# Turning the differences of the longest attention tiles by DMA, as two fp16 parts, in a fused attention and feed-forward layer

## The chip, the cores and the metric

The kernel runs on one core of a Trainium2 chip. The metric is the time of one execution on the device, in microseconds; the median of the runs counts. TensorE (PE in the profile) multiplies and transposes, VectorE (DVE), ScalarE (ACT) and GpSimd (POOL) do the elementwise work, SyncE (SP) issues most of the DMAs. Each engine runs its own instructions in order and waits on semaphores for the others.

## The reference

One transformer layer with differential attention (two softmax maps a head, of which the second is taken off with a factor), group norm, and a gated feed-forward part with ternary weights. B = 4 batches, T = 1024 positions, D = 512, H = 16 heads over KV = 4 key and value heads, E = 2048. Cut to what is computed:

```python
q1, q2 = rope(q[..., :32]), rope(q[..., 32:])      # of x @ Wq; k1, k2 in the same way of x @ Wk
s1 = einsum('bhtd,bhsd->bhts', q1, k1) * scale + mask
s2 = einsum('bhtd,bhsd->bhts', q2, k2) * scale + mask
diff = softmax(s1) - lam * softmax(s2)
out = einsum('bhts,bhsd->bhtd', diff, v)
out = group_norm(out) * (1 - LAMBDA_INIT)
x = layernorm(x + out @ Wo)
x = layernorm(x + (silu(x @ wu.T) * (x @ wg.T)) @ wd.T)   # wu, wg, wd: ternary
```

## The kernel before

The attention is cut into 512 tiles. Tile n has one head and 128 query positions; t from 0 to 7 says which, so that it sees t + 1 blocks of 128 keys. Sixteen tiles are a chunk (two heads, all t), 32 chunks make 4 batches, and tile 128 is the first of the second batch. The order of t (T_ORDER) puts a long tile (t = 7, 6, 5, 4; n even) beside a short one (n odd). r is 0 or 1, the two heads of a chunk; the tiles n and n + 2 of equal t are a "duo".

A tile goes through these steps: "scores" on PE for both maps (L1086); "minimum" on DVE for each, which copies the negated, masked scores to e1 or e2 and takes the row's extreme (L1443); "exponent" on ScalarE with the row sums (L1220); "factor" on GpSimd (L1368, L1369); "combine" on DVE, e1 + coef x e2 (L1514), the difference; "turn", transposes on PE of each block into a PSUM bank, four at most (L1067), and for r = 1 one more of "wide", the factors of the rows (L1071); "evict" on ScalarE from the bank to dt (L1210, L1213); "values" on PE, for each block one fp32 matmul with vkv for each head of the duo, whose outputs lie in the two halves of a bank (L1105); "product" on DVE (L1535). e1_long, e1_short and dt_short hold more than one tile, e2_long and e2_short one. dt_long has one place for each r.

Beside it run the "fills" on PE, cut into pieces: the projections of x (kinds E, O, V, two pieces each; L1125, L1132), the output projection with Wo (L1146), the transposes of its result (x1T, L1150), and the feed-forward jobs up, gate (L1159) and y (L1168). A batch's output projection and feed-forward part can start when its attention is complete, so those of the last batch stand in a tail behind all attention. The projections of later batches are spread over the time before.

What stands where on an engine is decided by a planner, `in_order`, when the program is built. It has a cost for each step (`takes`), what each step waits for (`after`), how long a DMA takes to land (`LANDS`), a preference (`AHEAD`), a pace (`PACE`: from tile 128 on, scores start no sooner than 16 x PACE after those of 16 tiles before, in the plan's time), and it lays out one fixed list for each engine. SP's list holds the loads of q (qstk, four places), k, v and weights, and the stores.

## Time and profile before

| | us |
|---|---|
| median of 3 runs | 2203.38 |
| lowest, highest | 2203.05, 2204.61 |
| the profiled execution's own time | 2203.33 |
| its span in the profile | 2201.3 |
| PE busy | 2132.3 |
| DVE busy | 1684.0 |
| ACT busy | 1458.0 |
| POOL busy | 1193.6 |

The profile is of one execution. Busy times are of instructions alone, not of waits; a matmul counts with its latency, so that a PE that is called busy may still have small gaps. An fp32 matmul is recorded as two instructions, a transpose or an fp16 matmul as one. Idle time is put down to the instruction of another engine that ended last before it ended.

### The profile page before, as it was taken

What the parts mean: (1) busy time and instruction counts of PE and PEld (TensorE: products, weight loads), DVE (VectorE), ACT (ScalarE), POOL (GpSimd) and SP (SyncE); (2) the same over time, 40 slices, a digit from 0 to 9 for tenths busy, and PEclk for the clock granted to TensorE, in tenths of its full rate; (3) what the DMA queues carried; (4) which work ended last, traced back from release to release, by engine and by line L of the source; (5) the groups of instructions that cost most, each with busy time, mean ns of one, the idle gap of its engine ahead of it and who ended that gap; (6) DMA issues with size and microseconds to landing.
All of it is one profiled execution on the core that took longest, in us unless ns stands there. A gap on an engine that the chain in (4) does not pass through costs nothing. (4 is left out here: it accounts for less than half of the span.)

```text
span 2201.3 us, 41404 instructions
## 1 busy us (share of the span) xinstructions
PE 2132.3 (97%) x13442; PEld 1375.0 (62%) x13442; DVE 1684.0 (77%) x3701; ACT 1458.0 (66%) x3450; POOL 1193.6 (54%) x1919
## 2 busy tenths in 40 slices
PE   8999999999999999999999999999999999999998
PEld 4666666666666666666666666666666666644443
DVE  4888788889889888888878878888877888743333
ACT  0777777667777777778677767767677777722232
POOL 0577666677655745555545655665554555531232
PEclk9999999999999999999999999999999999999999
DMA  7676566857653422222532322342532112021000
GB/s 253 198 211 217 191 213 203 244 174 222 189 164 116 121 72 68 92 59 72 173 115 63 87 68 72 98 130 68 154 92 68 51 42 87 30 77 48 1 20 20
DMA packets 257427, 255.49 MB, mean 116 GB/s; under 512 B 31296, under 2 KB 199360, under 8 KB 255168
## 3 DMA queue, kind: packets, MB, share of 16 engines
q1 hardware_dynamic: 246016, 220.26, 33.3%
q10 hardware_dynamic: 11200, 32.58, 4.6%
q8 instruction: 112, 1.84, 0.4%
q14 instruction: 99, 0.81, 0.1%
HBM read 181.48 MB, written 71.30 MB: 115 GB/s over the span
## 5 line engine op out<-in xcount | busy, mean ns | idle before, releaser
L1368 POOL TENSOR_TENSOR linv<-lsum,powers 128x2 f32<-128x2 f32 x512 | 408.7, 798 | 425.2 <-ACT e_long L1220 341.4
L1220 ACT ACTIVATE e_long<-e_long,nmax 128x768 f32<-128x768 f32 (+3 forms) x512 | 504.9, 987 | 161.2 <-DVE nmax L1443 157.7
L1443 DVE CUSTOM_DVE_ANT_0 e_long<-PS,mask_b 128x768 f32<-128x768 f32 (+3 forms) x512 | 516.2, 1019 | 74.8 <-PE PS L1086 56.3
L1086 PE MATMUL PS<-kstk,qstk 128*128 128x384 f32 (+5 forms) x1536 | 473.2, 413 | 20.9 <-DVE nmax L1443 10.2
L1086 PEld LDWEIGHTS PS<-kstk,qstk 128*128 128x128 f32 x1536 | 269.3, 189 | 143.2 <-issue 79.5
L1210 ACT ACTIVATE dt_long<-PS 128x512 f32<-128x512 f32 (+3 forms) x544 | 259.5, 514 | 121.2 <-PE PS L1067 114.4
L1514 DVE SCALAR_TENSOR_TENSOR e_long<-e_long,coef 128x1024 f32<-128x1024 f32 (+3 forms) x256 | 276.4, 1080 | 82.2 <-POOL coef L1369 81.7
L1220 ACT ACTIVATE e_short<-e_short,nmax 128x384 f32<-128x384 f32 (+3 forms) x512 | 283.0, 557 | 11.4 <-DVE nmax L1443 10.6
L1381 POOL TENSOR_TENSOR hid<-th,hid 128x512 f16<-128x512 f32 x128 | 148.3, 1161 | 251.6 <-ACT hid L1262 131.2
L1369 POOL TENSOR_SCALAR coef<-lsum,linv,neglam 128x1 f32<-128x1 f32 x512 | 229.5, 448 | 53.4
L1067 PE MATMUL PS<-ident,e_long 128*128 128x128 f32 x1664 | 240.5, 276 | 11.3 <-DVE nmax L1443 4.7
L1443 DVE CUSTOM_DVE_ANT_0 e_short<-PS,mask_b 128x384 f32<-128x384 f32 (+3 forms) x512 | 236.7, 485 | 9.9 <-PE PS L1086 4.5
L1168 PE MATMUL PS<-down_t,hid 128*128 128x512 fp8e4 x1024 | 233.9, 379 | 0.0
L1067 PEld LDWEIGHTS PS<-ident,e_long 128*128 128x128 f32 x1664 | 196.4, 142 | 54.3 <-issue 13.8
L1105 PE MATMUL PS<-dt_long,vkv 128*64 128x128 f32 x3328 | 205.0, 274 | 0.0
L1125 PE MATMUL PS<-xT,wr 128*128 128x512 f32 x400 | 190.2, 603 | 7.4 <-DMA wr<-in_w_proj 5.7
L1159 PE MATMUL PS<-x_hi,up_t 128*128 128x512 f16 x512 | 195.3, 381 | 0.0
L1159 PE MATMUL PS<-x_lo,up_t 128*128 128x512 f16 x512 | 194.9, 381 | 0.0
L1159 PE MATMUL PS<-x_hi,gate_t 128*128 128x512 f16 x512 | 194.2, 379 | 0.1
L1159 PE MATMUL PS<-x_lo,gate_t 128*128 128x512 f16 x512 | 194.0, 379 | 0.0
L1210 ACT ACTIVATE dt_short<-PS 128x512 f32<-128x512 f32 (+3 forms) x256 | 121.3, 474 | 105.3 <-PE PS L1071 68.7
L1105 PEld LDWEIGHTS PS<-dt_long,vkv 128*64 128x64 f32 x3328 | 187.7, 138 | 0.3 <-issue 0.3
(125 smaller groups left out, 3345.6 us busy)
## 6 DMA issues: line engine op xcount, KB each, us to landing
qstk<-dq SPq DMA_DIRECT2D x512, 128.0 KB, 2.9
dq<-hl SPq DMA_DIRECT2D x25, 1024.0 KB, 4.9
wr<-in_w_proj ACTq DMA_DIRECT2D x48, 512.0 KB, 4.6
kstk<-dk SPq DMA_DIRECT2D x64, 256.0 KB, 5.1
da<-ra SPq DMA_DIRECT2D x32, 512.0 KB, 3.3
at_sb<-da SPq DMA_DIRECT2D x32, 512.0 KB, 4.1
wt<-in_w_up SPq DMA_DIRECT2D x16, 512.0 KB, 5.9
wt<-in_w_gate SPq DMA_DIRECT2D x16, 512.0 KB, 5.2
```

Source lines behind the costliest of these rows:

```text
L1067: last = nc.tensor.transpose(F[bank][:, k * P:(k + 1) * P], e1_of(n)[:, col:col + P], ident[:, :])
L1086: last = nc.tensor.matmul(slot[:, h, :], qstk[:, duo % 4, 2 * r + m, :].bitcast(F32R), kstk[:, g % 2, m, h * w:(h + 1) * w].bitcast(F32R), ...
L1105: last = nc.tensor.matmul(bank[64 * r:64 * r + 64, at:at + P], vkv[:, duo // 16 % 2, kb, :], dt_of(n)[:, kb, :], start=kb == 0, stop=kb == t)
L1125: last = nc.tensor.matmul(bank[:, :], wr[:, job.i % 2, c, at:at + P], x_part(job, c), start=c == 0, stop=c == DC - 1)
L1159: last = nc.tensor.matmul(bank[:, :], w[:, c, job.i * P:(job.i + 1) * P], part[:, c, job.h * BANK:(job.h + 1) * BANK], start=c == 0 and pa ...
L1168: last = nc.tensor.matmul(bank[:, :], hid[:, part, e, job.j * P:(job.j + 1) * P], down_t[:, 8 * job.i + e, :], start=e == 0 and part == 0, ...
L1210: copied = nc.scalar.activation(dt_of(n)[:, 4 * half:4 * half + here, :].rearrange("p k q -> p (k q)"), F[bank][:, 0:here * P], ACT.Copy)
L1220: nc.scalar.activation(e, e, ACT.Exp, bias=nmax[:, u % 8:u % 8 + 1], scale=-1.0, accum_out=lsum[:, n % 4, m:m + 1]).then_inc(s_exp, 1)
L1368: link(nc.gpsimd.tensor_tensor(linv[:, a % 8, :], lsum[:, a % 4, :], mone, ALU.pow))
L1369: nc.gpsimd.tensor_scalar(coef[:, a % 2:a % 2 + 1], lsum[:, a % 4, 0:1], linv[:, a % 8, 1:2], neglam[:, :], ALU.mult, ALU.mult).then_inc(s ...
L1443: nc.vector.tensor_tensor_reduce(out, slot, mask, -1.0, -NEG, ALU.add, ALU.min, nmax[:, u % 8:u % 8 + 1]).then_inc(s_negmax, 1)
L1514: nc.vector.scalar_tensor_tensor(e1_of(a)[:, 0:w], e2_of(a)[:, 0:w], coef[:, a % 2:a % 2 + 1], e1_of(a)[:, 0:w], ALU.mult, ALU.add).then_i ...
```

## The change

From tile 128 on, the tiles with t = 7 and t = 6 ("laid": 4 in each chunk, 96 in all) take another way from "combine" to "values":

- "upper" on ScalarE copies the difference e1 to fp16, into the memory of e2 ("parts"); "lower" on DVE subtracts it from e1 and writes the rest, fp16 too, behind it.
- "lay" on SP issues one transposing DMA for both parts, 2 x (t + 1) blocks of 128x128, from e2 to dt_long.
- The transposes of these tiles on PE and their evictions go; for r = 1 the transpose of "wide" and its eviction stay.
- "v upper" on ScalarE and "v lower" on GpSimd split the values of a key head into two fp16 parts (vparts), once for each of the 12 key heads from the second batch on.
- "values" makes, for each block and head, four fp16 matmuls in place of one fp32 matmul: two parts of v by two parts of the difference.
- e2_long gets a second place. For even tiles the second map's minimum waits for the tile four before, not two before: for its "lay" if it is laid, else for its "combine". The first map's minimum waits for "lower" of the tile four before in place of its "turn".
- qstk has three places, not four; coef four, not two; X_HOMES is 4, not 6, by which the last batch's halves of x share four places. PACE is 3.55, not 3.75.

```diff
+def laid(n):
+    return STEPS[n].t >= 6 and n >= 128
 def turns(n):
+    if laid(n):
+        return STEPS[n].r
     return (STEPS[n].t + STEPS[n].r) // 4 + 1
...
-X_HOMES = 6
+X_HOMES = 4
...
-    home = (4 * h + c + 4) % X_HOMES
-    return home, B - 1 if home < 4 else h
+    return c, B - 1 + h
...
+    elif what == "lay":
+        out = [ITEM("lower", a)]
+        if a >= 4:
+            out.append(ITEM("values", run_of(STEPS[a - 4].duo)))
+            if STEPS[a].r:
+                out.append(ITEM("product", STEPS[a - 4].duo))
...
         if b == 0 and a >= 4:
-            out.append(ITEM("turn", a - 4, turns(a - 4) - 1))
-        if b == 1 and a >= 2:
+            out.append(ITEM("lower", a - 4) if laid(a - 4) else ITEM("turn", a - 4, turns(a - 4) - 1))
+        if b == 1 and a % 2 and a >= 2:
             out.append(ITEM("combine", a - 2))
+        elif b == 1 and a >= 4:
+            out.append(ITEM("lay", a - 4) if laid(a - 4) else ITEM("combine", a - 4))
...
-PACE = 3.75
+PACE = 3.55
...
-        qstk = sb("qstk", [P, 4, 4, P])
+        qstk = sb("qstk", [P, 3, 4, P])
...
+        vparts = sb("vparts", [P, NT, 2, 64], F16)
...
-        e2_long = sb("e2_long", [P, T])
+        e2_long = sb("e2_long", [P, 2, T])
...
+            def lay(n):
+                sp.wait_ge(s_lower, count_laid(n))
+                if n >= 4:
+                    sp.wait_ge(s_pv, run_of(STEPS[n - 4].duo) + 1)
+                    if STEPS[n].r:
+                        multiplied(sp, STEPS[n - 4].duo)
+                sp.dma_start_transpose(blocks_laid(n), parts_of(n)).then_inc(s_laid[STEPS[n].r], 16)
...
+                    if laid(first):
+                        pe.wait_ge(s_vlower, duo // 16 - V_FIRST + 1)
+                        been_laid(pe, first)
+                        been_laid(pe, second)
...
+                    if laid(heads[0]):
+                        for kb in range(t + 1):
+                            for v in range(2):
+                                for part in range(2):
+                                    for r, n in enumerate(heads):
+                                        last = nc.tensor.matmul(bank[64 * r:64 * r + 64, at:at + P], vparts[:, kb, v, :],
+                                                                blocks_laid(n)[:, part * (t + 1) + kb, :],
+                                                                start=kb == 0 and v == 0 and part == 0,
+                                                                stop=kb == t and v == 1 and part == 1)
+                        continue
...
+                elif what == "upper":
+                    w = width(a)
+                    act.wait_ge(s_comb, a + 1)
+                    nc.scalar.activation(parts_of(a)[:, 0:w], e1_of(a)[:, 0:w], ACT.Copy).then_inc(s_upper, 1)
...
+                elif what == "lower":
+                    w = width(a)
+                    dve.wait_ge(s_upper, count_laid(a))
+                    nc.vector.tensor_tensor(parts_of(a)[:, w:2 * w], e1_of(a)[:, 0:w], parts_of(a)[:, 0:w], ALU.subtract)\
+                        .then_inc(s_lower, 1)
```

What stands where also moves, since the planner runs anew. Two places show it, both in chunk 16, the first of the third batch, whose first tiles are 256 (t = 7, r = 0) and 258 (t = 7, r = 1). On VectorE, before, from the combination of tile 258 to the second map's minimum of tile 260 (L1514 is a combination, L1443 a minimum, L1492 and L1498 are feed-forward jobs):

```order
L1514 SCALAR_TENSOR_TENSOR e_long<-e_long,coef 128x1024 [waits s_coef]
L1498 SCALAR_TENSOR_TENSOR th<-th,PS 128x512 [waits s_ffull,s_ffree1]
L1514 SCALAR_TENSOR_TENSOR e_short<-e_short,coef 128x128 [waits s_coef]
L1443 ISA e_long,nmax<-PS,mask_b 128x896 [waits s_score,s_tb]
L1443 ISA nmax 128x1
L1492 SCALAR_TENSOR_TENSOR th<-th,PS 128x512 [waits s_th]
L1443 ISA e_long,nmax<-PS,mask_b 128x896 [waits s_score,s_comb]
```

And now, from "lower" of tile 256 (L1639) to the same minimum (L1634 is a combination, L1563 a minimum, L1612 and L1618 are the feed-forward jobs):

```order
L1639 TENSOR_TENSOR e_long<-e_long 128x1024 [waits s_upper]
L1563 ISA e_long,nmax<-PS,mask_b 128x896 [waits s_score,s_lower]
L1563 ISA nmax 128x1
L1612 SCALAR_TENSOR_TENSOR th<-th,PS 128x512 [waits s_th]
L1618 SCALAR_TENSOR_TENSOR th<-th,PS 128x512 [waits s_ffull,s_ffree4]
L1634 SCALAR_TENSOR_TENSOR e_long<-e_long,coef 128x1024 [waits s_coef]
L1634 SCALAR_TENSOR_TENSOR e_short<-e_short,coef 128x128 [waits s_coef]
L1612 SCALAR_TENSOR_TENSOR th<-th,PS 128x512 [waits s_th]
L1618 SCALAR_TENSOR_TENSOR th<-th,PS 128x512 [waits s_ffull,s_ffree3]
L1563 ISA e_long,nmax<-PS,mask_b 128x896 [waits s_score,s_laid0]
```

The minimum of tile 260 now waits for the DMA that turned tile 256 (s_laid0), and between "lower" and it stand one minimum, two combinations and four feed-forward jobs.

On PE, before, the turn of tile 258 and the values of the duo (L1067 and L1071 are transposes, L1159 a gate job, L1105 values; an fp32 matmul is one row entry here):

```order
L1067 MATMUL PS<-ident,e_long 128x128 [waits s_ffree7,s_comb]
L1067 MATMUL PS<-ident,e_long 128x128 x3
L1067 MATMUL PS<-ident,e_long 128x128 [waits s_negmax]
L1067 MATMUL PS<-ident,e_long 128x128 x3
L1071 MATMUL PS<-ident,wide 128x128 [waits s_wide,s_negmax]
...
L1105 MATMUL PS<-dt_short,vkv 64x128 [waits s_ffree3,s_vin0,s_ffree7,s_ffree6,s_ffree2]
L1105 MATMUL PS<-dt_short,vkv 64x128 x7
L1105 MATMUL PS<-dt_long,vkv 64x128 x16
```

And now the same values (L1200 the short duo's in fp32, L1193 those of tiles 256 and 258 in parts), with the scores (L1167) and a piece of a projection (L1220) that stand ahead of them:

```order
L1167 MATMUL PS<-kstk,qstk 128x256 [waits s_negmax]
L1167 MATMUL PS<-kstk,qstk 128x256 [waits s_ffree7]
L1220 MATMUL PS<-xT,wr 128x512 [waits s_xin2]
L1220 MATMUL PS<-xT,wr 128x512 [waits s_xin3]
...
L1200 MATMUL PS<-dt_short,vkv 64x128 [waits s_laid0,s_vlower,s_laid1,s_ffree6,s_negmax,s_ffree1,s_vin1]
L1200 MATMUL PS<-dt_short,vkv 64x128 x7
L1193 MATMUL PS<-dt_long,vparts 64x128 x64
```

The eight transposes of tile 258 (and of 256) are gone, 16 fp32 matmuls have become 64 fp16 ones, and the values stand two tiles later, behind the scores of tile 263 in place of 261. Over the whole program, the pieces of projections (E, O, V) ahead of the first scores of tile 128 are 143 before and 118 now, and those between them and the last scores of tile 511 are 49 before and 74 now; the up and gate jobs between the same two are 178 before and 188 now.

## Rows read from the trace of the kernel before

**Rows 1.** The page, section 1: busy time, share of the span, instructions.

```profile
span 2201.3 us, 41404 instructions
...
PE 2132.3 (97%) x13442; PEld 1375.0 (62%) x13442; DVE 1684.0 (77%) x3701; ACT 1458.0 (66%) x3450; POOL 1193.6 (54%) x1919
```

**Rows 2.** Busy time of the engines in three stretches; clock, DMA share, GB/s.

```profile
core 0: us, PE busy (x) PEld busy (x) DVE busy (x) ACT busy (x) POOL busy (x), PEclk, DMA share, GB/s
28.00:510.00 482.00, 458.55 (x2773) 313.17 (x2772) 396.77 (x876) 328.40 (x806) 318.22 (x449) 0.99 0.67 209
510.00:1924.00 1414.00, 1383.13 (x9461) 927.66 (x9460) 1172.74 (x2640) 1050.88 (x2521) 800.68 (x1346) 1.00 0.33 98
1924.00:2201.00 277.00, 268.24 (x1166) 124.26 (x1164) 101.25 (x167) 77.22 (x123) 71.59 (x111) 0.99 0.10 33
```

**Rows 3.** The same view, chunk by chunk (four of them).

```profile
278.00:337.00 59.00, 53.17 (x336) 36.64 (x335) 47.35 (x107) 42.58 (x103) 39.09 (x57) 0.97 0.71 219
337.00:391.00 54.00, 51.99 (x334) 35.46 (x333) 44.48 (x104) 38.95 (x99) 38.99 (x54) 1.00 0.62 191
...
689.00:748.00 59.00, 55.13 (x354) 38.41 (x354) 52.49 (x113) 42.67 (x101) 39.26 (x54) 0.97 0.50 158
...
1041.00:1098.00 57.00, 57.00 (x374) 39.20 (x372) 46.27 (x109) 40.14 (x100) 33.24 (x62) 1.00 0.54 160
```

**Rows 4.** Who waited for whom, 510 to 1924 us: total, times, longest (us).

```profile
DVE e_long L1514 <- POOL coef L1369: 64.0, 69, 3.2
...
DVE e_long L1443 <- PE PS L1086: 43.7, 54, 2.4
...
PE PS L1105 <- ACT dt_long L1210: 7.4, 6, 1.9
```

**Rows 5.** The same view for the DMA queue of SP.

```profile
SPq L946 <- PE PS L1086: 674.9, 159, 15.4
```

**Rows 6.** Groups of instructions by form, 510 to 1924 us: transposes and evictions.

```profile
L1067 PE MATMUL PS<-ident,e_long 128*128 128x128 f32 x1248 | 178.4, 275 | 7.7 <-DVE e_long L1514 3.6 <-DVE nmax L1443 3.0 <-ACT dt_short L1210 0.7
...
L1210 ACT ACTIVATE dt_long<-PS 128x512 f32<-128x512 f32 x264 | 151.2, 589 | 91.1 <-PE PS L1067 90.4
```

**Rows 7.** The timeline near 1004 us: start, length (us), what.

```profile
1003.77 1.92 PE L1105 MATMUL PS<-dt_long,vkv 128*64 128x128 f32 x32
...
1006.71 0.92 PE L1067 MATMUL PS<-ident,e_long 128*128 128x128 f32 x7
```

**Rows 8.** The chain that ended last: start, length (us), what.

```profile
1966.30 27.47 PE PS L1146 x64
...
2112.02 27.63 PE PS L1159 x128
```

**Rows 9.** Groups by form, 510 to 1924 us: VectorE work and exponents.

```profile
L1220 ACT ACTIVATE e_long<-e_long,nmax 128x1024 f32<-128x1024 f32 x96 | 110.1, 1148 | 23.7 <-DVE nmax L1443 23.2
...
L1443 DVE CUSTOM_DVE_ANT_0 e_long<-PS,mask_b 128x896 f32<-128x896 f32 x96 | 102.2, 1085 | 9.1 <-PE PS L1086 8.9
...
L1514 DVE SCALAR_TENSOR_TENSOR e_long<-e_long,coef 128x1024 f32<-128x1024 f32 x48 | 61.4, 1280 | 30.4 <-POOL coef L1369 30.4
L1498 DVE SCALAR_TENSOR_TENSOR th<-th,PS 128x512 f32<-128x512 f32 x89 | 60.9, 684 | 21.6 <-PE PS L1159 20.2
...
L1514 DVE SCALAR_TENSOR_TENSOR e_long<-e_long,coef 128x896 f32<-128x896 f32 x48 | 54.9, 1143 | 16.5 <-POOL coef L1369 16.5
...
L1514 DVE SCALAR_TENSOR_TENSOR e_short<-e_short,coef 128x128 f32<-128x128 f32 x48 | 16.5, 344 | 2.9 <-POOL coef L1369 2.8
...
L1487 DVE SCALAR_TENSOR_TENSOR x_lo<-PS,x_hi 128x512 f16<-128x512 f32 x24 | 16.1, 683 | 0.9 <-ACT x_hi L1248 0.9
```

**Rows 10.** DMA issues: queue, count, KB each, median us from issue to landing.

```profile
qstk<-dq SPq DMA_DIRECT2D x512, 128.0 KB, 2.9
...
da<-ra SPq DMA_DIRECT2D x32, 512.0 KB, 3.3
at_sb<-da SPq DMA_DIRECT2D x32, 512.0 KB, 4.1
...
th<-in_lambda ACTq DMA_DIRECT2D x1, 64.0 KB, 9.2
```

More of the change, by code:

```diff
@@ L257, in takes @@
         return 0.13 + 0.00104 * width(a)
+    if what == "upper":
+        return 0.2 + 0.00084 * width(a)
+    if what == "lower":
+        return 0.13 + 0.00104 * width(a)
+    if what == "lay":
+        return 0.0025 * width(a)
     if what == "empty":
@@ L282, in after @@
             first, second = heads_of(duo)
-            out += [ITEM("load v", duo // 16), ITEM("evict", first, turns(first) - 1), ITEM("evict", second, turns(second) - 1)]
+            out.append(ITEM("evict", second, turns(second) - 1))
+            if laid(first):
+                out += [ITEM("v lower", duo // 16), ITEM("lay", first), ITEM("lay", second)]
+            else:
+                out += [ITEM("load v", duo // 16), ITEM("evict", first, turns(first) - 1)]
     elif what == "mean":
```

111 lines of the change are left out of this document (83 added, 28 removed).

## The prediction

> **What bounds the kernel now.** I read the page first: TensorE (PE) is busy for 97% of the 2201.3 us span, VectorE (DVE) for 77%, ScalarE for 66%, GpSimd for 54% [rows 1]. A busy PE counts the latency of each matmul, so I cut the span at two events: 510 us, where tile 128 (the first of batch 1, the first that the change touches) starts, and 1924 us, where the last scores are done. PE is busy for 458.6 of the 482 us ahead of tile 128, 1383.1 of 1414 in the middle, 268.2 of 277 in the tail [rows 2]. The middle is the stretch of the change, and DVE is busy there for 1172.7 us, 83%. Then I put shorter stretches of one chunk (16 tiles, 54 to 60 us) beside each other [rows 3]. Where DVE has 46.3 of 57 us, PE is busy throughout; where DVE has 52.5 of 59 us (89%), PE loses 3.9 us. And the chunk from 278 to 337 us takes 59 us although PE is busy for only 53.2: PE bounds most of the middle, and something else, the hand-over of a tile from engine to engine, bounds much of the first stretch. The waits say the same: in the middle DVE waits 64.0 us for GpSimd's factors and 43.7 us for scores, the longest that PE itself waits for is 7.4 us, for evictions [rows 4].
>
> **What leaves PE.** A long tile of t = 7 or 6 has 8 or 7 blocks of 128 keys; 24 chunks x 2 x (8 + 7) = 720 of the 1248 transposes of long tiles in the middle go [rows 6]. Seven of them took 0.92 us [rows 7], the last with its latency of 0.275 [rows 6], so one costs (0.92 - 0.275) / 6 = 0.108 us, and 720 cost 78 us of PE time.
>
> **What comes to PE.** The values of such a pair of tiles took, for each block, four fp32 matmul records of 128 columns, two heads side by side on the array: 32 records in 1.92 us, (1.92 - 0.27) / 30 x 2 = 0.110 us for two records, 0.22 us for a block of both tiles. Now a block takes four pairs of fp16 matmuls. A 512-column fp32 record costs 27.47 / 64 = 0.429 us, an fp16 one 27.63 / 128 = 0.216 us, half as much [rows 8]. So an fp16 pair of 128 columns should cost half of 0.110, and four of them 0.22 us again: 360 blocks, 0 to +2 us. Nothing here shows fp16 matmuls of 128 columns with two heads side by side, nor instructions following each other twice as fast as in [rows 7]. The other end is that a pair keeps its 0.110 us: 0.44 us a block, 360 x 0.22 = +79 us. I take the low end, since at 512 columns the halving is exact. Removed from PE: 78 - 1 = 77 us. The Trainium skill (TensorE: Matmul & The Clock Gate, Back-to-back issue gap) gives about 81 ns for each matmul of 128 columns in a stream with its weight loads; by it a block would take 8 x 0.081 = 0.65 us, and the values 155 us more. The trace disagrees: its fp32 records already follow every 0.055 us.
>
> **Where that time goes.** A fixed order is made for each engine, and it moves too. Counted in the order: ahead of tile 128 there were 143 pieces of the projections, now 118; in the middle 25 more, and 10 more up and gate jobs, which stood in the tail. A piece is four fp32 records, 1.72 us; an up or gate job eight fp16 ones, 1.73 us. So PE's work changes by -43 us in the first stretch, by -77 + 43 + 17 = -17 us in the middle and by -17 us in the tail, -77 in all.
>
> First stretch: nothing of the new path runs there, only work is taken out. The chunks of 278 to 337 and of 337 to 391 us show that PE's load doesn't set the length: 53.2 us busy in 59, 52.0 in 54 [rows 3]. Ends: 0 and -43 us. I take -8, as 29 of the 32 chunks take 56.5 to 61 us whatever PE carries.
>
> Middle: DVE gets 96 subtractions ("lower") of up to 1024 fp32 values. The nearest rows are the combinations of the same tiles, 1.280 and 1.143 us [rows 9]; an fp16 result doesn't make DVE faster here (0.683 us for 512 elements, as for fp32). 48 x (1.280 + 1.143) = 116 us, 4.8 us a chunk. With about 20 us for the jobs moved in, DVE has 1172.7 + 116 + 20 = 1309 us to do in 1414 - 17 = 1397: 94%. A chunk that had 46 to 48 now has 51 to 53, as in the chunks of 89% in [rows 3], where PE lost 3 to 4 us. Ends: 0, and 24 x 3.9 = +94 us. Against it stand waits that go: ScalarE waited 90.4 us for transposes ahead of its long evictions [rows 6] and PE 7.4 for those evictions [rows 4]; the second map's minimum no longer waits for the tile just before it, since e2_long is double. I take +9 us. The middle: -17 + 9 = -8.
>
> Tail: PE is dense there, jobs taken out shorten it: -17.
>
> ScalarE: in a chunk seven evictions of 512 columns (0.589 us each [rows 6]) and one of 384 go, over 4.1 us; the four copies to fp16 ("upper") have no row of their own, the exponents of 1024 take 1.148 [rows 9], so at most 4.6 us. Nothing either way. The 12 "v upper" on ScalarE and 12 "v lower" on GpSimd are of 512 elements each, on engines that idle a quarter of the middle or more [rows 2]: nothing. Three places for q in place of four: a q load still starts some three tiles (3 x 1414 / 384 = 11 us) ahead and lands in 2.9 us [rows 10], and SP spends 675 us of the middle waiting for scores ahead of these loads [rows 5]: nothing. X_HOMES 4: the last batch's second half waits for its first; at most one landing, 5 to 9 us if nothing covered it, and the order has other pieces there.
>
> The transposing DMA ("lay") is the new link, on SP's queue; behind it stand q loads and other loads, which have tiles of margin. It must land before DVE's minimum of the second map four tiles on. In the order quoted, DVE has between them: one minimum (1.085), four jobs of 0.684, a combination of 1.280 and one of 0.344 [rows 9], 5.4 us, and about 5.0 where they overlap a little. No row shows such a DMA. Plain ones of 512 KB land in 3.3 us (from SBUF) and 4.1 us (into SBUF in rows of 512 bytes), the slowest of any in 9.2 [rows 10]. I take 4.1, the nearest, so that it lands under that cover; past 5.0 us each microsecond costs up to 96 us in all. The values on PE come later still, so PE isn't first to wait.
>
> **Sum.** -8 - 8 - 17 = -33 us on 2203.3 (the profiled execution: span 2201.3 and 2.0 around it, equal to the median of 2203.4): **2170 us**, its own range 2150 to 2190.
>
> **Rivals.**
> 1. PE bounds everything and all of its 77 us count: 2203 - 77 = 2126. For it: 97% busy. Against it: [rows 3], and 43 of the 77 us lie where PE wasn't the bound. Chance 0.15; up to 2150.
> 2. DVE takes it all back: it is as full as in the 89% chunks everywhere, which costs 24 x 1 to 2 us more than I took: 2190 to 2208. For it: 94% is more than any stretch shows. Chance 0.18.
> 3. Slower, by the landing of the transposes. If one takes 6.5 us from issue to landing, DVE stands still for 1.5 us at up to 96 places, 144 us at most; half of it hidden gives 2170 + 72 = 2242, and PE waits behind. It decides from 5.0 us on. For it: 46 MB more (24 x 1.92) in 16-bit pieces, which no row shows; against it: DMA engines are a third busy in the middle [rows 2]. Chance 0.22. The Trainium skill (VectorE: DVE Perf Modes, The three transpose paths) gives 1309 ns for one 128x128 block by DMA; 16 of them one after another are 21 us, and the kernel would be far slower than any time here. Its page DMA: Bandwidth & Descriptors (Latency and other measured facts) gives 261 GB/s for such DMAs, 2 us for 512 KB, and by it this rival falls. No run here shows either yet.
> 4. Slower, by the fp16 matmuls: a pair keeps 0.110 us, PE's work is +79 where I put +1; the middle grows, 2170 + 60 to 2170 + 78 = 2230 to 2248. For it: instructions would have to follow at twice the rate of [rows 7]. Chance 0.08.
> My forecast has 0.37.
>
> **How the numbers follow.** A measurement tells 0.2%, 4.4 us, from no change. Faster than 2199: 0.37 + 0.15 + 0.07 of rival 2 = 0.59. Within 0.2%: 0.09 of rival 2 and 0.01 of rival 3 = 0.10. Slower: 0.02 + 0.21 + 0.08 = 0.31. From 2135 to 2255 lie the forecast, rival 2, rival 4, half of rival 1 and two thirds of rival 3: 0.37 + 0.18 + 0.08 + 0.07 + 0.14 = 0.84.
>
> **What the changed profile would show.** The first scores of tile 128 at about 502 us: right for the first stretch; 467 would speak for rival 1. Transposes of long tiles in the middle: 528 for 1248. 64 fp16 value matmuls in about 1.9 us: right; 3.5 is rival 4. The "lower" rows at 1.1 to 1.3 us and DVE over 90% busy in the middle. The transposing DMA with 4 to 5 us to landing, and DVE's minima with hardly any wait on it; waits of 1 us and more there are rival 3. A tail near 260 us. I am wrong if the first stretch shrinks with its load, if DVE can't be kept 94% busy, or if the DMA lands past 5 us.

## The result, and the profile after

| | before | after |
|---|---|---|
| median, us | 2203.99 (4 runs) | 2257.91 (4 runs) |
| lowest, highest | 2203.05, 2210.01 | 2248.79, 2261.49 |
| span of the profiled execution | 2201.3 | 2255.2 |

The ratio is 1.0232, with a 95% interval of 1.0197 to 1.0268: slower by 54 us, where I had forecast 33 us faster. The time is 3 us above the range of 2135 to 2255.

In the changed kernel L1563 is the minimum, L1634 the combination, L1376 "upper", L1639 "lower", L1047 "lay", L1148 a turn, L1167 the scores, L1193 the fp16 values, L1200 the fp32 values, L1004 the store of rotated projections. Its page and three stretches as in [rows 1, 2], cut at its own events (tile 128 at 515 us, the last scores at 1992), columns as there:

```profile
PE 2109.6 (94%) x14162; PEld 1321.8 (59%) x14162; DVE 1799.2 (80%) x3797; ACT 1472.6 (65%) x3390; POOL 1247.7 (55%) x1931
```

```profile
28.00:515.00 487.00, 437.50 (x2650) 296.48 (x2649) 378.25 (x846) 327.95 (x804) 279.75 (x427) 0.96 0.61 184
515.00:1992.00 1477.00, 1398.21 (x10379) 898.62 (x10378) 1313.48 (x2775) 1072.99 (x2475) 898.93 (x1386) 0.98 0.53 134
1992.00:2255.00 263.00, 251.45 (x1090) 116.79 (x1088) 94.16 (x156) 70.14 (x111) 65.91 (x105) 0.99 0.11 35
```

The first stretch is 5 us longer, though PE is busy for 21 us less in it. The middle is 63 us longer. The tail is 14 us shorter. The granted clock is new: a mean of 0.994 over the span before and 0.976 now (the view of spans and clocks, before and then after):

```profile
core 0: 2201.3 us, clock 0.994
```

```profile
core 0: 2255.2 us, clock 0.976
```

The clock has two levels, 2.4 and 1.2 GHz. It was at the lower one for 24 us before and for 109 us now. PE was busy in 20 and in 87 us of these, and half of that is lost: 10 and 44 us. (While PE stands, a lower clock costs nothing.) With that I can split the time from 28 us on. PE's work at full clock is its busy time less the loss, and the rest is idle:

| us | window | PE's work at full clock | lost to the clock | PE idle |
|---|---|---|---|---|
| before | 2173 | 2100 | 10 | 63 |
| after | 2227 | 2044 | 44 | 140 |
| difference, first stretch | +5 | -33 | +12 | +26 |
| difference, middle | +63 | -6 | +21 | +48 |
| difference, tail | -14 | -17 | 0 | +3 |
| difference, all | +54 | -56 | +33 | +77 |

So work left PE, 56 us of the 77 that I had forecast. Idle time and a slower clock took 110 us, twice that.

Where? The parts of the change as it is written show no fault of that size. First the groups by form from 515 to 1992 us (columns as in [rows 6]), then the DMA by its line, and the timeline of a pair's values:

```profile
L1193 PE MATMUL PS<-dt_long,vparts 128*64 128x128 f16 x2880 | 91.8, 223 | 0.0
...
L1148 PE MATMUL PS<-ident,e_long 128*128 128x128 f32 x523 | 78.5, 278 | 4.0 <-DVE e_long L1634 1.9 <-DVE x_lo L1607 1.0 <-ACT dt_long L1308 0.7
...
L1639 DVE TENSOR_TENSOR e_long<-e_long 128x1024 f16<-128x1024 f32 x48 | 66.6, 1386 | 5.0 <-ACT e_long L1376 4.8
...
L1639 DVE TENSOR_TENSOR e_long<-e_long 128x896 f16<-128x896 f32 x48 | 59.6, 1242 | 2.4 <-ACT e_long L1376 2.4
```

```profile
L1047 SPq DMA_TRANSPOSE dt_long<-e_long x96: 1295/1855/8627, 529.0 to 1972.3; - x96
...
  DVE e_long L1563: 30.4, 12
  PE PS L1200: 15.4, 5
...
DMA to landing us min/median/max: 3.9/4.3/11.5
```

```profile
933.71 1.96 PE L1193 MATMUL PS<-dt_long,vparts 128*64 128x128 f16 x64
```

The transposes of long tiles are down to 523 records (528 in the order). 64 fp16 value matmuls take 1.96 us. "Lower" takes 1.39 and 1.24 us where I took 1.28 and 1.14, 126 us in all. The DMA lands in 4.3 us in the middle case, but one took 11.5, and DVE waited 30 us for it in 12 places.

The lengths of the chunks (from the first minimum of one to that of the next) show that the loss isn't spread:

| us | before | after |
|---|---|---|
| chunks 1 and 2, first batch, nothing laid | 117.7 | 136.1 |
| chunks 0 and 3 to 7, first batch, nothing laid | 339.8 | 327.4 |
| chunks 8 to 11 | 238.4 | 275.3 |
| chunk 17 | 56.8 | 78.2 |
| mean of the other chunks from 12 on | 59.0 | 59.3 |
| from the start of chunk 31 to the end | 333.7 | 319.3 |

Chunks 9 and 17 in the view of busy times, columns as in [rows 2]:

```profile
582.00:650.00 68.00, 60.40 (x378) 36.62 (x378) 60.23 (x120) 45.44 (x100) 44.55 (x63) 0.95 0.70 186
...
1084.00:1162.00 78.00, 66.28 (x417) 42.72 (x416) 57.50 (x122) 40.26 (x95) 46.65 (x70) 0.91 0.65 183
```

DVE is 89% and 74% busy, PE 89% and 85%: neither is full, each waits for the other or for a DMA. A full DVE isn't what makes a chunk long: chunk 21 has DVE busy for 53.7 of 57 us, 94%, and takes no longer than before.

```profile
1337.00:1394.00 57.00, 56.19 (x432) 35.60 (x432) 53.70 (x114) 44.89 (x107) 35.21 (x52) 1.00 0.39 99
```

In chunk 17 the chain that ended last (start, length, what) shows what such a pile-up is:

```profile
1094.73 1.28 POOL t L1508
1096.01 2.23 POOL t L1510
...
1103.40 1.23 POOL hl L1516
1104.63 2.22 POOL hl L1518
1106.85 0.02 issue
1106.87 0.38 SPq L1004
...
1108.24 8.49 DMA dt_long<-e_long
1116.73 0.24 issue
1116.98 1.98 PE PS L1200 x16
1118.95 3.29 PE PS L1193 x64
```

GpSimd finishes a rotated projection. SP's list holds its 1 MB store ahead of the lay, and the lay, issued after it, lands only 8.5 us later. Below are the stretches while PE stood and just after (the view of busy times; the last three columns are clock, DMA share, GB/s):

```profile
1084.00:1110.00 26.00, 25.83 (x137) 14.69 (x136) 23.86 (x49) 16.29 (x37) 18.80 (x29) 1.00 0.41 119
1110.00:1116.70 6.70, 1.39 (x4) 0.32 (x2) 3.52 (x6) 2.72 (x4) 4.36 (x5) 0.88 1.12 274
1116.70:1123.00 6.30, 6.02 (x86) 5.93 (x87) 2.75 (x7) 1.49 (x3) 1.28 (x3) 0.58 1.08 343
```

PE stood for 5.6 us, and then the granted clock was 0.58. The 64 value matmuls, 1.96 us at full clock, took 3.3 us. Here the stall cost more than its length. The stalls come first elsewhere in this trace too: ahead of each of the 18 falls of the clock between 28 and 2250 us, PE had idled for 1.8 to 4.7 us of the last 7, where the mean of the whole is 0.4. So what the clock took came behind the stalls.

### The profile page after: what moved, and what is told of

It is laid out like the page before. It is cut to its first block, busy times and chain, and to the rows that moved or that the text cites. A ratio compares the mean times of both kernels' runs of the same rounds, so it can differ in the third digit from the quotient of the medians.

```text
span 2255.2 us, 43097 instructions
## 1 busy us (share of the span) xinstructions
PE 2109.6 (94%) x14162; PEld 1321.8 (59%) x14162; DVE 1799.2 (80%) x3797; ACT 1472.6 (65%) x3390; POOL 1247.7 (55%) x1931
## 4 chain that ended last, share of the span: by engine, by line
PE 55%; DVE 8%; DMA 4%; issue 4%; POOL 4%; ACT 2%; SPq 0%; DVEq 0%; POOLq 0%; ACTq 0%
PE PS L1254 15%; PE PS L1241 8%; PE PS L1263 8%; PE PS L1167 7%; PE PS L1200 5%; PE PS L1148 4%; DMA dt_long<-e_long 4%; PE PS L1220 4%; PE PS L1193 3%; DVE e_long L1563 2%; DVE e_long L1634 1%; POOL linv L1475 1%; PE PS L1227 1%; DVE e_long L1639 1%; PE PS L1152 1%
## 5 line engine op out<-in xcount | busy, mean ns | idle before, releaser
L1563 DVE CUSTOM_DVE_ANT_0 e_long<-PS,mask_b 128x768 f32<-128x768 f32 (+3 forms) x512 | 516.5, 1019 | 83.0 <-PE PS L1167 36.1
L1167 PE MATMUL PS<-kstk,qstk 128*128 128x384 f32 (+5 forms) x1536 | 481.0, 417 | 54.6 <-DVE nmax L1563 34.5
L1167 PEld LDWEIGHTS PS<-kstk,qstk 128*128 128x128 f32 x1536 | 269.3, 192 | 195.0 <-issue 87.2
L1634 DVE SCALAR_TENSOR_TENSOR e_long<-e_long,coef 128x1024 f32<-128x1024 f32 (+3 forms) x256 | 276.2, 1079 | 29.1 <-POOL coef L1476 28.4
L1493 POOL TENSOR_TENSOR hid<-th,hid 128x512 f16<-128x512 f32 x128 | 160.6, 1261 | 214.3 <-ACT hid L1360 131.9
L1476 POOL TENSOR_SCALAR coef<-lsum,linv,neglam 128x1 f32<-128x1 f32 x512 | 236.0, 461 | 53.4
L1563 DVE CUSTOM_DVE_ANT_0 e_short<-PS,mask_b 128x384 f32<-128x384 f32 (+3 forms) x512 | 238.2, 486 | 14.7 <-PE PS L1152 6.7
L1220 PE MATMUL PS<-xT,wr 128*128 128x512 f32 x400 | 193.0, 613 | 6.5 <-DMA wr<-in_w_proj 5.6
L1308 ACT ACTIVATE dt_long<-PS 128x512 f32<-128x512 f32 (+3 forms) x328 | 150.9, 499 | 39.1 <-PE PS L1148 35.7
L1263 PEld LDWEIGHTS PS<-down_t,hid 128*128 128x128 f16 x1024 | 98.9, 99 | 111.3 <-issue 6.5
L1148 PE MATMUL PS<-ident,e_long 128*128 128x128 f32 x944 | 145.5, 283 | 17.6 <-ACT dt_short L1308 4.3
L1634 DVE SCALAR_TENSOR_TENSOR e_short<-e_short,coef 128x128 f32<-128x128 f32 (+3 forms) x256 | 139.8, 546 | 22.6 <-POOL coef L1476 21.9
L1360 ACT ACTIVATE hid<-th 128x512 f16<-128x512 f32 x128 | 80.2, 627 | 95.2 <-DVE th L1618 95.0
```

The source lines that it names most:

```text
L1148: last = nc.tensor.transpose(F[bank][:, k * P:(k + 1) * P], e1_of(n)[:, col:col + P], ident[:, :])
L1167: last = nc.tensor.matmul(slot[:, h, :], qstk[:, duo % 3, 2 * r + m, :].bitcast(F32R), kstk[:, g % 2, m, h * w:(h + 1) * w].bitcast(F32R), ...
L1220: last = nc.tensor.matmul(bank[:, :], wr[:, job.i % 2, c, at:at + P], x_part(job, c), start=c == 0, stop=c == DC - 1)
L1263: last = nc.tensor.matmul(bank[:, :], hid[:, part, e, job.j * P:(job.j + 1) * P], down_t[:, 8 * job.i + e, :], start=e == 0 and part == 0, ...
L1308: copied = nc.scalar.activation(dt_of(n)[:, 4 * half:4 * half + here, :].rearrange("p k q -> p (k q)"), F[bank][:, 0:here * P], ACT.Copy)
L1476: nc.gpsimd.tensor_scalar(coef[:, a % 4:a % 4 + 1], lsum[:, a % 4, 0:1], linv[:, a % 8, 1:2], neglam[:, :], ALU.mult, ALU.mult).then_inc(s ...
```

## The experiments

Each was timed beside runs of the kernel before (medians of 2202 to 2204 us). The ratios are to those.

**The side changes, and the load on each engine alone.** e1_side is the changed kernel with no tile laid and the pace of before.

```diff
 def laid(n):
-    return STEPS[n].t >= 6 and n >= 128
+    return False
-PACE = 3.55
+PACE = 3.75
```

> The changed kernel without a single laid tile, and with the pace of before: what is left of the change are three places for q, the second place of e2_long with its looser waits, four places for x, and the planner's new order. Theory V (in the changed kernel VectorE bounds the middle: it can't be kept busier than about 91%, and a chunk takes its VectorE work over 0.91): VectorE's work is that of before, so 2203 within 10 us. Theory O (the moved order is the loss: 25 pieces of projections taken out of the first stretch, which doesn't shrink, and put into the middle): 2215 to 2240, with the first scores of tile 128 near 515 us as in the changed kernel.

2275.73 us, ratio 1.0328 (1.0307 to 1.0349): 72 us slower than before, more than either theory had, and 18 us slower than the whole change. So the side changes with their order cost more than all that the change loses. But they don't lose it in the same places. Of the 72 us, 41 are behind the start of chunk 31 (374.4 us for 333.7), where the changed kernel is 14 us shorter: the planner puts only 161 up and gate jobs in the middle here, 178 before and 188 in the changed kernel. So the 18 us aren't a clean price of the laid path. Chunks 1 and 2 are as long as in the changed kernel (136.1 us), so that loss belongs to the side changes. Chunk 17 is not (59.3 us for 78.2), and chunks 8 to 11 take 247 us, between 238 and 275.

e2_dve is the kernel before with one more subtraction on DVE for each of the 96 tiles.

```diff
+                    if extra(a):
+                        dve.wait_ge(s_comb, a + 1)
+                        nc.vector.tensor_tensor(e2_of(a)[:, 0:w].bitcast(F16)[:, 0:w], e1_of(a)[:, 0:w],
+                                                e2_of(a)[:, 0:w], ALU.subtract).then_inc(s_extra, 1)
```

> The kernel before with one more subtraction on VectorE behind each combination of the 96 tiles that the change takes (same size as lower; its result is not used). Work on PE and all orders are those of before. VectorE's work in the middle goes from 1173 to 1285 us. Theory V: 1285 / 0.91 = 1412 us for the middle, so little is lost, 2203 to 2225, with VectorE at 90 to 91%. If each microsecond of VectorE counted in full: 2310. If PE alone bounded: 2203 to 2208.

2276.27 us, ratio 1.0328 (1.0313 to 1.0344). DVE's busy time is 108 us more (1792.2 us for 1684.0) and the time 72 us, where theory V had 0 to 22: each microsecond on DVE costs two thirds of one, spread evenly (62.1 us a chunk for 59.0). The price has in it that each subtraction waits for the combination ahead of it to complete. PE was called 97% busy, and yet DVE's load counts.

```profile
PE 2151.4 (95%) x13442; PEld 1375.8 (60%) x13442; DVE 1792.2 (79%) x3797; ACT 1460.5 (64%) x3450; POOL 1224.9 (54%) x1919
```

e6_turn_short is the kernel before with one transpose where a turn of those tiles had up to four.

```diff
-                for k in range(keys):
+                for k in range(min(keys, 1) if STEPS[n].t >= 6 and n >= 128 else keys):
```

> The kernel before with one transpose in place of up to four in each turn of the same 96 tiles (the rest of the difference is left out): 528 transposes less, 57 us of PE work, nothing added, same orders. If PE bounds the middle: 2203 - 57 = 2146 to 2155. If the hand-over from engine to engine and VectorE do: 2190 or more. Theory V allows 2146, as 1173 / 0.91 is below 1414.

2188.11 us, ratio 0.9930 (0.9915 to 0.9946). 528 transposes of 0.108 us are 57 us of PE's time; its busy time fell by 44 us (2088.1 for 2132.3), and 16 came out. A microsecond off PE is worth 0.28 to 0.36 of one. My steps had priced PE and DVE the other way round.

```profile
PE 2088.1 (96%) x12914; PEld 1318.6 (60%) x12914; DVE 1683.8 (77%) x3701; ACT 1456.1 (67%) x3450; POOL 1200.9 (55%) x1919
```

e3_lower_short is the changed kernel with "lower" cut to its first 128 columns on DVE; ScalarE fills the second part instead.

```diff
-                    nc.vector.tensor_tensor(parts_of(a)[:, w:2 * w], e1_of(a)[:, 0:w], parts_of(a)[:, 0:w], ALU.subtract)
+                    nc.vector.tensor_tensor(parts_of(a)[:, w:w + P], e1_of(a)[:, 0:P], parts_of(a)[:, 0:P], ALU.subtract)
```

> The changed kernel, same orders, with lower cut to 128 columns on VectorE, and ScalarE copying the difference a second time in its place (the second part is thus wrong). VectorE's work in the middle falls from 1324 to about 1225 us, ScalarE's rises by about 100. Theory V: chunks fall to what PE and the hand-overs need, 2190 to 2215. Theory O (queues and the moved pieces): 2240 to 2255, as the changed kernel.

2238.76 us, ratio 1.0168 (1.0145 to 1.0191): 19 us under the changed kernel, just below what theory O had. Its group now takes 40.9 us:

```profile
L1640 DVE TENSOR_TENSOR e_long<-e_long 128x128 f16<-128x128 f32 x96 | 40.9, 426 | 32.1 <-ACT e_long L1377 32.0
```

So 85 us off DVE's "lower" gave 19. That is no price of DVE's time by itself, since DVE now waits 32 us for ScalarE's second copy, where it waited 7. Chunks 8 to 11 stay at 270.7 us and chunk 17 at 77.1: the length of "lower" on DVE isn't what makes the pile-ups.

**Which side change.** e4_q3 is the kernel before with three places for q, in the memory, the waits and the plan.

```diff
-        if a >= 4:
-            out.append(ITEM("scores", heads_of(a - 4)[1], 1))
+        if a >= 3:
+            out.append(ITEM("scores", heads_of(a - 3)[1], 1))
...
-        qstk = sb("qstk", [P, 4, 4, P])
+        qstk = sb("qstk", [P, 3, 4, P])
...
-                if duo >= 4:
-                    sp.wait_ge(s_score, 2 * heads_of(duo - 4)[1] + 2)
+                if duo >= 3:
+                    sp.wait_ge(s_score, 2 * heads_of(duo - 3)[1] + 2)
```

> The kernel before with one side change alone: three places for q, so that a load of q waits for the scores of the duo three back, not four; the planner runs anew (132 pieces of the projections ahead of tile 128 for 143, 169 up and gate jobs in the middle for 178). Theory Q (the loss of 72 us by the side changes is the later loads of q and the order that follows from them): 2245 to 2275, with the tail 20 to 40 us longer. Theory W (it is the second place of e2_long with its looser waits, which lets the planner set up another order): 2204 to 2215 here. If both share it, 2220 to 2240.

2232.16 us, ratio 1.0134 (1.0119 to 1.0149). e5_wait is the other side change:

```diff
-        if b == 1 and a >= 2:
-            out.append(ITEM("combine", a - 2))
+        if b == 1 and a % 2 and a >= 2:
+            out.append(ITEM("combine", a - 2))
+        elif b == 1 and a >= 4:
+            out.append(ITEM("combine", a - 4))
...
-        e2_long = sb("e2_long", [P, T])
+        e2_long = sb("e2_long", [P, 2, T])
```

> The kernel before with the other side change: e2_long and coef have twice the places, even tiles' second minimum waits for the combination of the tile four before, X_HOMES is 4 (which alone leaves the order as it was); q keeps four places. The planner puts 127 pieces ahead of tile 128 (143 before) and 173 up and gate jobs in the middle (178). Theory W: 2245 to 2275, most of the 72 us. Theory Q: 2204 to 2215, since nothing waits longer than before. By the number of pieces alone (11 and 16 fewer ahead of tile 128) both would lose, 20 to 45 us each.

2235.11 us, ratio 1.0155 (1.0138 to 1.0172). Neither theory stands alone: they cost 30 and 33 us, within the 20 to 45 that the count of moved pieces had given. A wait that was made looser costs as much as one that was made tighter, which speaks for the order in both. For the looser wait that stays an argument. For q's places e16_order_alone tests it: the kernel before with four places and its own waits, but all lists in the order of e4_q3. Only the planner's two lines of the diff of e4_q3 are in it.

> The kernel before, in its memory and its waits (four places for q, a load waits for the scores of the duo four back), but with all engines' lists in the order that the planner makes for three places, the same as in e4_q3 (2232). If the order costs and not the wait: 2228 to 2236, with a tail (from the start of the last chunk) of 360 to 370 us for 334. If the wait for a free place costs: 2203 to 2212.

2227.69 us, ratio 1.0114 (1.0099 to 1.0129). The order alone costs 25 of e4_q3's 30 us. It brings tile 128 forward to 491 us from 510, with 11 fewer pieces of projections ahead of it; they fill the middle, 9 up and gate jobs are pushed behind it, and from the start of chunk 31 to the end it takes 366 us for 334. The first stretch gains 19 us, the chunks from 8 to 30 lose 11 and the end loses 32. The 11 pieces are 19 us of PE's work, so here the first stretch did shrink with its load. The 5 us between this run and e4_q3 fit the wait for a place: in e4_q3 PE waits 9.2 us for loads of q, and before not at all.

```profile
PE PS L1086 <- DMA qstk<-dq: 9.2, 6, 3.9
```

e17_before_pace asks the same of a number that only the planner reads.

```diff
-PACE = 3.75
+PACE = 3.65
```

> The kernel before with pace 3.65 for 3.75 and the planner run anew: 161 up and gate jobs in the middle for 178, the first batch as before. If a plan's slack alone moves the time: the 17 jobs go to the tail, which grows by 17 x 1.73 = 29 us, and the middle shrinks by no more than 10, so 2212 to 2232. If PE's work is only moved about: within 5 us of before.

2219.78 us, ratio 1.0076 (1.0059 to 1.0092). Chunk 31 starts 21 us earlier and the end is 40 us longer. The 17 jobs, 29 us of PE's work, aren't saved but done later, and there they cost 40 us where the middle gives back 21. e8_pace is the changed kernel with PACE 3.75 for 3.55.

> The changed kernel with the pace of before, 3.75 for 3.55, so that the plan gives the chunks after tile 128 61 us, not 57; the planner sets 118 pieces ahead of tile 128 as now, 192 up and gate jobs in the middle for 188. Theory O (DVE can't keep the tighter plan, so chunks come out as they like): within 5 us of the changed kernel, 2250 to 2262, but the chunks even. If the tighter pace caused the pile-ups in chunks 8 to 11 and 17, these fall to 60 to 64 us and the whole to 2225 to 2240. If the pace bound, it would be 5 to 15 us slower.

2261.41 us, ratio 1.0275 (1.0248 to 1.0302), nothing that differs from the changed kernel by more than the runs spread. Chunk 17 falls to 59.0 us, but chunks 8 to 11 take 279.6 and the others 60.6 each. The tight pace was not the cause of the loss.

**The DMA.** e7_plain copies the same bytes without turning them.

```diff
-                sp.dma_start_transpose(blocks_laid(n), parts_of(n)).then_inc(s_laid[STEPS[n].r], 16)
+                sp.dma_start(blocks_laid(n), parts_of(n).rearrange("p (k q) -> p k q", q=P)).then_inc(s_laid[STEPS[n].r], 16)
```

> The changed kernel with each transposing DMA in place of it a plain copy of the same bytes from parts to dt_long; nothing is turned, so the values are made of wrong numbers; all else and all orders stay. Theory T (the transposing form is slow to issue, 1.3 to 1.9 us on SP, and lands late when DMA engines are 70 to 80% busy, which holds up DVE for 30 us and PE for 15): issue under 0.7 us, landing 3 to 4 us, chunks 9, 10, 11 and 17 shrink by 5 to 15 us each, the whole 2215 to 2235. Theory O (the new order with its heavy chunks sets the time, not the DMA): the same chunks stay at 66 to 78 us, the whole 2245 to 2258.

2239.45 us, ratio 1.0167 (1.0148 to 1.0185): 18 us less, between the two. By its line, and who waited:

```profile
L1047 SPq DMA_DIRECT2D dt_long<-e_long x96: 495/510/710, 528.4 to 1956.9; - x96
...
DMA to landing us min/median/max: 2.7/3.1/11.8
```

```profile
DVE e_long L1563 <- DMA dt_long<-e_long: 12.7, 6, 7.4
...
PE PS L1200 <- DMA dt_long<-e_long: 11.9, 4, 6.4
```

The turning form costs 1.3 us more of SP's queue for each and 1.2 us more to land. Yet a plain copy lands as late as 11.8 us too, chunks 8 to 11 keep 263.3 us of 275.3 and chunk 17 keeps 76.3. So the pile-ups don't come from the form alone. That the late landings come from other traffic is a guess that fits the DMA share of 1.12 in the stretch of the stall; no run tests it.

**The laid path with the first batch as it was.** e9_first_as_before puts q's fourth place into the memory of vparts until tile 128, and keeps the old wait of the second minimum up to tile 131.

```diff
+def q_place(duo):
+    return duo % 4 if duo < 64 else duo % 3
+def q_back(duo):
+    return 4 if duo < 64 else 3
...
-        if a >= 3:
-            out.append(ITEM("scores", heads_of(a - 3)[1], 1))
+        if a >= q_back(a):
+            out.append(ITEM("scores", heads_of(a - q_back(a))[1], 1))
...
-        if b == 1 and a % 2 and a >= 2:
+        if b == 1 and (a % 2 or a < 132) and a >= 2:
```

> The changed kernel with its two side effects on the first batch taken back: q keeps a fourth place until tile 128 (it lies where vparts lies later), and the second map's minimum of even tiles waits as before up to tile 131; from there on all is as in the changed kernel. The planner then has 142 pieces ahead of tile 128 (143 before, 118 in the changed kernel) and 192 up and gate jobs in the middle. Theory O (most of the loss is the order that the planner makes under three places for q and the looser waits, above all in the first batch): the first scores of tile 128 at 505 to 512, the pile-ups of chunks 1, 2 and 8 to 11 smaller, the whole 2205 to 2230. Theory L (the laid path loses the time by itself, through VectorE's load and the DMA's landing): 2240 to 2258, since the laid path is as it was.

2206.25 us (10 runs), ratio 1.0008 (0.9995 to 1.0021): 52 us of the 54 are gone, by an edit that alters no step of the laid path. But all lists move with it, in the middle too: 24 of the 25 pieces go back ahead of tile 128. Only 10 of the 52 us are gained ahead of tile 128 (505.5 us for 515.4). Chunks 8 to 11 give 6, chunk 17 gives 7, and the other chunks from 12 on, which no longer carry the pieces, give 29 (57.7 us each for 59.3). e10_none_laid is the same kernel with laid() false and PACE 3.75.

> The kernel of e9_first_as_before with no tile laid (pace 3.75 as before), so that only three places for q and the looser waits are left, both from tile 128 on; 142 pieces ahead of tile 128, 176 up and gate jobs in the middle (178 before). Theory O: the order ahead of tile 128 is nearly that of before, so 2204 to 2220, where the side changes from the start gave 2276. If the looser waits and the three places cost in the middle by themselves: 2240 to 2270. The distance from here to e9_first_as_before is what the laid path is worth by itself: -15 to -30 us by theory O, +10 to +40 by theory L.

2209.19 us (10 runs), ratio 1.0020 (1.0010 to 1.0029), where the same side changes from the start (e1_side) had 2275.73. So theory O stands for most of the loss. But the laid path on this ground is worth 3 us, not 15 to 30. The two kernels also differ in the pace, 3.55 and 3.75 (192 and 176 up and gate jobs in the middle), and a tenth of pace alone moves other kernels here by 17 and 21 us, so the 3 us are uncertain by about as much. The split shows why (e9_first_as_before, then e10_none_laid, sums of the view of busy times from 28 to 2204 us):

```profile
sum 2176.00, PE 2060.20 PEld 1303.23 DVE 1778.45 ACT 1463.45 POOL 1239.82; mean PE 686.73 PEld 434.41 DVE 592.82 ACT 487.82 POOL 413.27
```

```profile
sum 2176.00, PE 2113.97 PEld 1367.81 DVE 1673.12 ACT 1459.40 POOL 1178.93; mean PE 704.66 PEld 455.94 DVE 557.71 ACT 486.47 POOL 392.98
```

With the clock counted as above (58 and 29 us busy at the lower level), PE's work is 2031 against 2099 us, 68 less, where I had forecast 77. It loses 15 us more to the clock and stands idle for 54 more, and that is the 68 again. DVE has 105 us more to do. Chunks 8 to 11 (269.1 us for 244.1) and 17 (70.9 for 57.6) are 38 us longer. The chunks from 12 on without 17 give 21 back (57.7 us each for 58.8) and the end 18.

e11_t7 lays only the tiles of t = 7 (48).

> The kernel of e9_first_as_before with only the tiles of t = 7 laid, 48 for 96; 160 up and gate jobs in the middle. Theory L (each laid tile adds 1.1 to 1.3 us to a full VectorE, and PE gets back 0.6 to 0.7 us of it): faster than e9_first_as_before by 10 to 20 us. Theory O: the laid path gains by itself, so half of it gains half: slower by 5 to 15 us, also because 32 up and gate jobs go back to the tail.

2221.63 us, ratio 1.0066 (1.0044 to 1.0088), 15 us slower than e9_first_as_before. Its chunks are the shortest of all (56.9 us), but with 32 fewer up and gate jobs in the middle the end takes 378.1 us for 320.5. The order weighs more than the question I had put, so of the worth of one laid tile this run tells little.

e12_own_queue is e9_first_as_before with the stores of rotated projections issued by ScalarE.

```diff
+                elif what == "store rotated":
+                    store_rotated(act, a)
```

> The kernel of e9_first_as_before with the stores of the rotated projections (1 MB each) issued by ScalarE, not by SP, so that no transposing DMA stands in SP's list behind a store that waits for GpSimd. Theory H (the pile-ups of chunks 8 to 11 and 17 come of this place in the list): the chunks over 62 us in the middle shrink to 58 to 61 us, SP's waits for lower of 3 us and more stay, waits of VectorE and PE for the transposing DMA fall from 45 us in all to under 15, the whole 15 to 30 us below e9_first_as_before. If it is the traffic itself (both use the same 16 DMA engines) or VectorE's load, within 6 us of it.

2226.25 us, ratio 1.0093 (1.0073 to 1.0114), slower by 20 us, which neither side of the expectation had. PE's waits for a lay grow from 9.5 to 19.1 us, chunks 8 to 11 stay at 269.2. Theory H isn't borne out: that a lay stands behind a store in SP's list is what the chain shows, but taking the store out of that list didn't help. The planner's new order is in this result too, so the queue isn't priced by itself.

**Away from the ternary weights.** In chunks 8 to 11 DVE also prepares the ternary weights (the last step at tile 184). e13_from_192 is e9_first_as_before with laid tiles from chunk 12 on.

```diff
-    return STEPS[n].t >= 6 and n >= 128
+    return STEPS[n].t >= 6 and n >= 192
```

> The kernel of e9_first_as_before with tiles laid from tile 192 (chunk 12) on, not from 128, 80 for 96. In chunks 8 to 11 VectorE also prepares the ternary weights (up to tile 184). Theory C (the laid tiles' subtractions collide there with that preparation, VectorE is full, PE stands and its clock falls): chunks 8 to 11 at 57 to 62 us for 63 to 77, PE's mean clock 0.987 or more for 0.982, the whole 2206 - 30 + 13 (what 16 laid tiles gave) = 2180 to 2195. If the gain is lost all along the middle: 2203 to 2215.

2187.96 us, ratio 0.9929 (0.9910 to 0.9948), in the expected 2180 to 2195: **the fastest kernel here, 15.6 us under the one before.** Chunks 8 to 11 take 234.2 us for 269.1, chunk 17 takes 60.5, and DVE's waits for a lay are down to 5 us. First chunk 9 of e9_first_as_before, then of e13_from_192 (columns as in [rows 2]):

```profile
569.00:646.00 77.00, 57.89 (x363) 38.11 (x363) 60.55 (x118) 43.94 (x97) 50.79 (x64) 0.82 0.65 179
```

```profile
569.00:629.00 60.00, 51.76 (x317) 35.10 (x316) 51.49 (x109) 40.12 (x93) 40.77 (x56) 0.91 0.59 185
```

```profile
DVE e_long L1584 <- DMA dt_long<-e_long: 4.9, 7, 1.3
```

In chunks 8 to 11 it has nothing laid, so their shortening shows that the laid tiles lengthened them, and not which of their neighbours did it. It has as many up and gate jobs in the middle as e10_none_laid, 176, and is 21 us faster: where they don't pile up, 80 laid tiles may be worth about that (the paces differ, 3.55 and 3.75).

e14_from_192_pace gives it the pace 3.65, so that 192 up and gate jobs stand in the middle for 176.

> The kernel of e13_from_192 with pace 3.65 for 3.55, for which the planner puts 192 up and gate jobs in the middle, not 176, and evens the plan (59 to 61 us a chunk, three over 61). Theory C: pile-ups come where the plan asks more of VectorE than it can do, so an even plan gains a little: 0 to 10 us below e13_from_192. If the pace binds, 5 to 10 us above.

2208.95 us (10 runs), ratio 1.0019 (1.0007 to 1.0030): 21 us slower, against both expectations. The end is 13 us shorter (323.8 for 336.6), but the chunks from 12 on take 59.8 us each for 58.0. With e17_before_pace, which lost 17 us by the reverse, it says that one number of the planner moves the time by as much as the whole idea, and not in one direction. A kernel with tiles laid from tile 256 on (e15_from_256) gave no time, so that the laid tiles of chunks 12 to 15 have no price of their own.

## Why the prediction was wrong

**What leaves PE, what comes to PE: right in the main.** 64 fp16 matmuls take 1.96 us, and 56 us of work are gone; 68 between e10_none_laid and e9_first_as_before, against the forecast of 77. Rival 4, the fp16 pair that keeps its 0.110 us, falls. The Trainium skill (TensorE: Matmul & The Clock Gate, Back-to-back issue gap) has about 81 ns for a matmul of 128 columns. The trace disagrees: one starts every 0.03 us here, two side by side.

**Middle, -8 forecast, +63 measured: the step that failed most is the worth of the laid path.** In the sum it stood at -68 us: PE's 77 us counted whole, and +9 for the 116 us of DVE's "lower" less the waits that go. The other parts of the sum are the moved order: -8 + 43 + 17 - 17 = +35. The runs put the laid path at +3 (e9_first_as_before against before), -3 (against e10_none_laid) and -18 (the changed kernel against e1_side), with the orders and paces that differ in each, and nowhere near -68. They put the moved order at +52 (the changed kernel against e9_first_as_before). So of the 87 us between forecast and result some 70 are the laid path and 17 the order; by e1_side it would be 50 and 37. The parts don't add up exactly, but by either the laid path is the larger.

I had priced PE's microsecond at 1 and DVE's at under 0.1, the waits that go taken off. e6_turn_short puts PE's at 0.28 to 0.36 and e2_dve puts DVE's at 0.67. In the trace, PE's own work in the middle fell by 6 us (-17 forecast), but it stood idle for 48 more and the clock, for which the sum had no term, took 21. DVE got 126 us of "lower" for 116, and 1313 us in all, near my 1309. It was 89% busy over the middle and not 94, though single chunks reached 94. The two prices by themselves would make the laid path +51 (105 us more on DVE, 68 less on PE), and it came out at -3. Why is not shown: the planner knew of the work, ScalarE's long evictions went, and DVE's waits for the factors of long tiles fell from 64.0 [rows 4] to 10.8 us.

**First stretch: -8 forecast between 0 and -43, +5 measured.** I had the row for the load and left out that the order in which the rest stands changes too. Chunks 1 and 2 went from 117.7 to 136.1 us, with nothing laid in them, and the others gave 12 us back. PE's work fell by 33 us, but it stood for 26 more and lost 12 more to the clock. e1_side shows that the side changes alone do it. Nor is it so that the load doesn't count: in e16_order_alone 11 pieces less made the stretch 19 us shorter. (The row behind my -8 was read a little high too: 28 of the first 31 chunks take 56.5 to 61 us.)

**"Three places for q ... nothing", "the second map's minimum no longer waits": too low.** As waits they were nearly right: the one for a place of q is worth some 5 us (e4_q3 less e16_order_alone). But each changes the planned order. That costs 25 us for q's places (shown by e16_order_alone), 33 for the looser wait with its order, 72 for both with the rest (e1_side). I had counted the order of the whole, 25 pieces out of the first stretch and 10 more jobs in the middle, and given it +35.

**The transposing DMA: right in the middle case, wrong in the spread.** I took 4.1 us and a cover of 5.0; the median is 4.3. Rival 3 (landing past the cover at up to 96 places) forecast about 2242 by a loss everywhere. What happened was 12 places on DVE with 30 us and 5 on PE with 15, up to 7 us each. Replacing the form by a plain copy gave 18 us. The rival is right in sign and a third of the story. The Trainium skill (VectorE: DVE Perf Modes, The three transpose paths) has 1309 ns for one block; 14 or 16 blocks land in 4.3 us here, so the figure can't be added up for one DMA. The Trainium skill (DMA: Bandwidth & Descriptors, Latency and other measured facts) has 261 GB/s, by which 512 KB would take 2 of the 4.3 us.

**Tail: -17 forecast, -14 measured.** Right, and it is no gain of its own: the work stood in the middle.

**What stays open.** Why PE stands just enough in chunks 8 to 11 is shown by taking the laid tiles away, not by taking the ternary steps away. It may be DVE's load, the busy share of the DMA engines there, or both (that share is 0.69 to 0.80 in the changed kernel, 0.43 in chunk 12). The share alone doesn't do it: in the kernel before, chunk 8 has 0.79 and takes 59 us, with PE busy for 55.4.

```profile
510.00:569.00 59.00, 55.41 (x359) 39.39 (x358) 52.59 (x112) 44.44 (x104) 44.80 (x60) 1.00 0.79 239
```

Chunk 17 piles up too and has no ternary steps. What makes some of the DMAs land late, and why the prices of PE and DVE don't add up, stays open as well. The rank of the kernels within some 20 us is as much the planner's as the idea's: no run holds one order fixed with and without laid tiles.

## What to carry to other kernels

Where a planner or a fixed order stands behind a kernel, a change of memory or of a wait is a change of the whole order: build the kernel with the side changes alone and time it before believing in the main one. Price a microsecond on each engine by a run (one added on DVE cost 0.67, one taken off PE gave 0.28 to 0.36), not by which engine is called 97% busy. And try a new path in one stretch after another: the same code from tile 192, with the first batch left alone, turned +54 us into -16. DVE, which it loads, was 88 to 90% busy in the chunks from 8 to 11 before and 75 to 86% in most of those behind; that this is the reason wasn't tested.

## What the runs showed of the hardware

- One transposing DMA of 14 or 16 fp16 blocks of 128x128 (448 or 512 KB) takes 1.86 us of SP's queue to issue in the median, up to 8.6, and lands in 4.3 us, up to 11.5; a plain copy of the same bytes takes 0.51 and 3.1.
- fp16 matmuls of 128 columns by 64, two heads side by side on the array, follow each other every 0.03 us (64 in 1.96 us), fp32 records every 0.055 [rows 7].
- The granted clock fell after PE had stood for 5.6 us, and 64 matmuls took 3.3 us for 1.96. In the changed kernel the clock was at its lower level for 109 us, in 87 of which PE was busy: 44 us of work lost, for 10 before. PE had idled for 1.8 to 4.7 us shortly ahead of each fall.
- The subtraction of 1024 values from fp32 to fp16 took DVE 1.39 us in the mean, the combination of the same tiles, all fp32, 1.28 [rows 9]; over both widths one took from 1.04 to 2.20. What makes the slow ones slow wasn't tried.
